# Squares of the gated tile: from GpSimd to the scalar engine in a state-space loop

## The reference, cut to what matters

```python
y = _ssd(x, Bm, Cm, D, dt, dt_bias)          # 128 heads of 64: 8192 channels
yg = y * jax.nn.silu(gate)
yg_g = yg.reshape(Bsz, S, NG, GROUP)         # 8 groups of 1024 channels
rstd = jax.lax.rsqrt(jnp.mean(jnp.square(yg_g), axis=-1, keepdims=True) + EPS)
out = (yg_g * rstd).reshape(Bsz, S, INTER) * norm_w
return out @ out_proj_w.T
```

## Time and profile before

| | |
|---|---|
| median of 3 runs | 2258.87 us (2258.38 to 2261.21) |
| the profiled execution | 2256.16 us, its span 2253.9 us |
| mean granted clock of PE | 0.987 of full speed |
| busy: PE, DVE, ACT, POOL | 2149.1, 1676.1, 1434.7, 1038.2 us |
| stages, us from the span's start | expert and attention blocks to about 550, first SwiGLU and the set-up of the loop to about 595, loop to about 2032, its end to about 2062, second SwiGLU to 2254 |

### The profile page before, as it was taken

One profiled execution on the slowest core, in us unless ns is written; L12 is line 12 of the kernel. 1 busy time (PEld: TensorE's weight loads), 2 busy tenths in 40 slices (PEclk: granted clock), 3 DMA queues, 4 the chain that ended last, 5 costly groups with the idle time before them and its releaser, 6 DMA issues. The chain is left out here.

```text
span 2253.9 us, 34737 instructions
## 1 busy us (share of the span) xinstructions
PE 2149.1 (95%) x12556; PEld 1748.4 (78%) x12556; DVE 1676.1 (74%) x2693; ACT 1434.7 (64%) x3086; POOL 1038.2 (46%) x759
## 2 busy tenths in 40 slices
PE   7889989999899999999999999999999999997999
PEld 7856677887688878878887887887887888785887
DVE  7667755133688898889889889889988988986221
ACT  4377734333877677677777767766877677673332
POOL 5466535443146344444435533634445443545442
PEclk9999999999999999999999999999999999998999
DMA  3000012331333233223322323223322322231332
GB/s 131 1 1 1 1 43 61 94 94 57 141 113 108 94 117 122 85 86 140 122 85 85 141 94 113 97 94 129 107 100 85 141 108 100 85 113 40 92 95 83
DMA packets 64151, 202.50 MB, mean 90 GB/s; under 512 B 7024, under 2 KB 8048, under 8 KB 55664
## 3 DMA queue, kind: packets, MB, share of 16 engines
q1 hardware_dynamic: 63984, 200.31, 25.9%
HBM read 197.39 MB, written 2.88 MB: 89 GB/s over the span
## 5 line engine op out<-in xcount | busy, mean ns | idle before, releaser
L529 POOL TENSOR_TENSOR wAl<-rawA,wAh 128x512 fp32r<-128x512 f32 x233 | 325.8, 1411 | 406.1 <-ACT wAh L670 405.4
L1599 PE MATMUL ps<-xTh,wAh 128*128 128x512 f32 x1512 | 427.3, 404 | 7.9 <-DVE oacc L1437 3.0
L1599 PE MATMUL ps<-xTl,wAh 128*128 128x512 f32 x1512 | 415.0, 396 | 0.0
L1599 PE MATMUL ps<-xTh,wAl 128*128 128x512 f32 x1512 | 413.9, 395 | 0.0
L1332 DVE SCALAR_TENSOR_TENSOR work<-ps,chp,work 128x510 f32<-128x510 f32 (+2 forms) x465 | 343.5, 744 | 51.6 <-ACT work L829 41.6
L1599 PEld LDWEIGHTS ps<-xTl,wAh 128*128 128x128 f32 x1512 | 284.9, 188 | 69.7
L1599 PEld LDWEIGHTS ps<-xTh,wAh 128*128 128x128 f32 x1512 | 276.6, 189 | 78.4 <-issue 17.5
L1599 PEld LDWEIGHTS ps<-xTh,wAl 128*128 128x128 f32 x1512 | 283.6, 188 | 69.3
L535 POOL TENSOR_TENSOR wBl<-rawB,wBh 128x512 fp32r<-128x512 f32 x108 | 142.2, 1330 | 386.1 <-ACT wBh L674 386.1
L866 ACT ACTIVATE eb<-eb,gc 128x128 f32<-128x128 f32 x1008 | 307.7, 391 | 18.0 <-DMA eb<-scr_decays 18.0
L579 POOL TENSOR_TENSOR sqt<-gt 128x512 f32<-128x512 f32 x112 | 154.4, 1379 | 120.6 <-DVE gt L1391 112.1
(11 more groups left out here) (202 smaller groups left out, 3958.5 us busy)
## 6 DMA issues: line engine op xcount, KB each, us to landing
eb<-scr_decays SPq DMA_DIRECT2D x63, 1536.0 KB, 6.4
rawA<-ma_in SPq DMA_DIRECT2D x144, 256.0 KB, 3.6
rawA<-fa_in SPq DMA_DIRECT2D x88, 256.0 KB, 2.6
rawB<-mb_in SPq DMA_DIRECT2D x64, 256.0 KB, 2.8
rawB<-fb_in SPq DMA_DIRECT2D x44, 256.0 KB, 2.6
x<-x_in SPq DMA_DIRECT2D x8, 256.0 KB, 6.2
x_out<-x SPq DMA_DIRECT2D x8, 256.0 KB, 2.7
wqraw<-wqkv_in SPq DMA_DIRECT2D x1, 1536.0 KB, 10.9
```

The source lines that it names most:

```text
L529: nc.gpsimd.tensor_tensor(wAl[:, slot, :], rawA[:, slot, :], wAh[:, slot, :].bitcast(F32), ALU.subtract).then_inc(A_lo, 1)
L1599: return nc.tensor.matmul(o, l, r, start=start, stop=end, **kw)
```

## The change

The squares leave POOL. A new function on ACT, `y_square`, writes them into `sqt` behind each `y_hi`, after a wait until POOL has added up the square before it. POOL's `square` only adds `sqt` to `sq` (or copies it, for v = 0). Two moves go with it: in odd steps POOL's `lo_B` pair goes from ahead of the two additions to behind them, and in `finish` the four `lo_A` and the `lo_B` for the second SwiGLU go from ahead of both squares to behind the second one. `y_lo`, `taps`, PE's order and all DMAs stay as they are.

```diff
--- before.py
+++ after.py
@@ -567,17 +567,13 @@
 
         def square(v, g, p):
 
-            pool.wait_ge(m_yg, 2 * (g * TPG + v) + p + 1 + FREE)
             half = slice(512 * p, 512 * p + 512)
-            y = gt[:, v % 2, half]
+            pool.wait_ge(m_sqt, 2 * (g * TPG + v) + p + 1)
             if v == 0:
                 pool.wait_ge(m_ss, g + FREE)
-                nc.gpsimd.tensor_tensor(sq[:, half], y, y, ALU.mult).then_inc(m_sq, 1)
+                nc.gpsimd.tensor_copy(sq[:, half], sqt[:, :]).then_inc(m_sq, 1)
             else:
-                k = g * 2 * (TPG - 1) + 2 * (v - 1) + p + 1
                 pool.wait_ge(m_sq, 2 * (g * TPG + v) + p + FREE)
-                nc.gpsimd.tensor_tensor(sqt[:, :], y, y, ALU.mult).then_inc(m_sqt, 1)
-                pool.wait_ge(m_sqt, k)
                 nc.gpsimd.tensor_tensor(sq[:, half], sq[:, half], sqt[:, :], ALU.add).then_inc(m_sq, 1)
 
         def rstd_of(g):
@@ -588,13 +584,13 @@
         def step(v, g, last=False, first=False):
             for i in step_tiles(v, last):
                 lo_A(A0G + i, g, NA_G)
-            if v % 2 == 1:
-                lo_B(B0G + v + 1, g, TPG)
-                lo_B(B0G + v + 2, g, TPG)
             if v == 0 and not first:
                 rstd_of(g - 1)
             square(v, g, 0)
             square(v, g, 1)
+            if v % 2 == 1:
+                lo_B(B0G + v + 1, g, TPG)
+                lo_B(B0G + v + 2, g, TPG)
 
         def last_rstd(p):
             pool.wait_ge(m_var, NG + p + FREE)
@@ -603,12 +599,12 @@
                                     ALU.pow).then_inc(m_rstd, 1)
 
         def finish():
+            square(TPG - 1, NG - 1, 0)
+            last_rstd(0)
+            square(TPG - 1, NG - 1, 1)
             for u in range(4):
                 lo_A(A0F + u)
             lo_B(B0F)
-            square(TPG - 1, NG - 1, 0)
-            last_rstd(0)
-            square(TPG - 1, NG - 1, 1)
             for t in range(AHEAD):
                 layer_rstd(5, t)
             last_rstd(1)
@@ -880,6 +876,12 @@
             nc.scalar.activation(yTh[:, v % 2, half], gt[:, v % 2, half], ACT.Copy,
                                  scale=param(0, 2 + 2 * v, 6)).then_inc(m_yhi, 1)
 
+        def y_square(g, v, p):
+            k = 2 * (g * TPG + v) + p
+            act.wait_ge(m_yg, k + 1 + FREE)
+            act.wait_ge(m_sq, k + FREE)
+            nc.scalar.activation(sqt[:, :], gt[:, v % 2, 512 * p:512 * p + 512], ACT.Square).then_inc(m_sqt, 1)
+
         def step(v, g, last=False, first=False):
 
             gn, todo = step_chunks(v, g, last)
@@ -912,7 +914,9 @@
                 conv_silu(gn, conv[1])
                 conv_start(gn, conv[3], slot)
                 y_hi(g, v, 0)
+                y_square(g, v, 0)
                 y_hi(g, v, 1)
+                y_square(g, v, 1)
                 conv_silu(gn, conv[2])
                 conv_start(gn, conv[4], slot)
                 conv_silu(gn, conv[3])
@@ -940,7 +946,9 @@
                 hi_A(A0F + u)
             hi_B(B0F)
             y_hi(NG - 1, TPG - 1, 0)
+            y_square(NG - 1, TPG - 1, 0)
             y_hi(NG - 1, TPG - 1, 1)
+            y_square(NG - 1, TPG - 1, 1)
             normalise(5, 0)
             for t in range(1, AHEAD):
                 normalise(5, t)
```

## The result

The changed kernel takes 2290.24 us (median of 4 runs, 2289.49 to 2290.47) against 2259.57 us (median of 4, 2258.38 to 2261.21): ratio 1.0135 (95% interval 1.0123 to 1.0148), 30.7 us slower. The profiled execution took 2290.11 us, its span is 2288.3 us, the mean granted clock 0.985.

A forecast was written before the change was run, and what follows sets the result against it. TensorE, busy 95% of the span, was taken as the bound. The terms 27 + 2 + 1.3 - 3 + 4 + 0 + 4 gave 35 us over 2258.87, so 2294 us, range 2265 to 2322.

The forecast's parts named there:

- odd steps v = 3 and 5: Steps v = 3 and v = 5 of eight groups: 1.7 us slower each, 27 us in all (bounds 6 and 42).
- step v = 1: First odd step: later in front, earlier at the decay pair; 2 us for groups 1 to 7, 1.3 for group 0.
- even steps: POOL's multiplications leave y_lo and decay_off, most of PE's waits for decay matrices go: -3 us.
- step v = 7: Squares between conv_start and conv_silu may make taps(3) and chunk 6 late: 0.6 us in 7 groups, 4 us.
- end of the loop: PE's sums start about 5 us sooner, but splits now stand ahead of layer_rstd: gain given back, 0 us.
- clock: New waits of PE bring part of the time at 1.2 GHz: 4 us added (bounds 0 and 15).
- The square between the two y_hi: ACT in odd steps: the square moves y_hi(1), and with it y_lo(1), by 0.6 us.
- The additions' new place: Odd steps, beside DVE: the first addition costs y_lo(1) 0.15 us, the second costs the decay_off pair 1.08 us.
- Only the order on ACT: Additions miss DVE's two-input instructions, only the square's 0.6 us counts in odd steps: 2271 us, chance 0.17.
- Faster: Additions fall into DVE's pauses, and DVE, freed from 112 multiplications beside it, shortens PE's waits: 2245 us, chance 0.11.
- No change: Small losses in odd steps made up by v = 1, even steps and the end: within 4.5 us of 2259, chance 0.09.
- ACT as the bound: 128 squares add 81 us to ACT, busy 1434.7 of 2254 us; counted inside the forecast, no chance of its own.

The follow-up runs named there:

- e1: Changed kernel with POOL's additions and copies into sq replaced by memsets that read nothing, the sums of squares left out: 2248.46 us, ratio 0.9955.
- e6: Kernel before with only the change's finish order (squares and last_rstd ahead of the four lo_A and the lo_B): 2257.22 us, ratio 0.9991.
- e7: Kernel before with finish reordered: squares and last_rstd first, each layer_rstd followed by one lo_A, lo_B last: 2254.46 us, ratio 0.9979.
- e4: Kernel before with only POOL's lo_B pair moved behind the squares in odd steps, all squares still on POOL: 2307.33 us, ratio 1.0220.
- e9: Changed kernel with both y_hi ahead of the first square on ACT in steps 1, 3 and 5: 2271.21 us, ratio 1.0050.
- e5: Changed kernel, odd steps: ACT's squares behind the exponentials and behind hi_B, POOL's lo_B pair between the additions: 2255.85 us, ratio 0.9986.
- e3: Changed kernel, steps 1, 3, 5: POOL's additions back behind the lo_B pair, ACT's second square behind hi_B, first square unmoved: 2277.56 us, ratio 1.0081.

## Why the prediction was right, step by step

The time, 2294 us, was 4 us above the measured one. The mechanism came out as written: the square ahead of y_hi(1), the addition beside decay_off, PE's new wait at t = 3 of steps 3 and 5, 16 times. The sum, 35 us, agrees with the 34.4 us between the two spans, but that is in part luck, since errors of both signs stand behind it:

| step of the prediction | priced | measured |
|---|---|---|
| odd steps v = 3 and 5 | 27 | 31.7: 1.63 a step in nine, 2.4 in seven |
| step v = 1, group 0 | 1.3 | 3.9 |
| step v = 1, groups 1 to 7 | 2 | -1.4 |
| even steps | -3 | -5.1 (-5.3 of it in v = 2) |
| step v = 7 | 4 | 4.4 |
| end of the loop | 0 | +0.1 |
| clock | 4 | about -3 in the loop, inside the rows above |

*The square between the two y_hi* was priced 0.6 and lasts 0.622 us. It moves y_hi(1) by only 0.51 (1.61 us behind y_hi(0), before 1.10) and the second y_lo by 0.52 against PE's first output product, where 0.6 or more had been written. PE's restart costs 0.10 (0.73 instead of 0.63), not 0.02. The two errors cancel: less the margin the square costs 0.47 us in e1, and the sum had 0.45.

*The additions' new place.* The second addition beside decay_off was priced 1.08: the pair went from 1.29 to 2.38 us, and stays at 1.29 in e1. The first was priced 0.15 and cost y_lo 0.08 us in v = 5. In seven of the eight steps v = 3 it cost 0.56 us (1.31 against 0.75), since DVE enters them late; these steps also had no margin left before the change, and the wait for the decay pair adds 0.31 us. Taking v = 5 as the pattern for v = 3 made this term too small by some 5.4 us; v = 5 itself was a little cheaper than priced (1.63 against 1.7), so in all it is 4.7 us short. The rows also show who waits for whom, which I had left open. In v = 5 the second addition starts at 1470.12, 0.33 us behind the decay_off pair, and ends at 1471.62; that it takes 1.50 us instead of 1.28 (the half of the B splits' 2.55) is its own wait for the first decay_off. The second decay_off ends at 1472.17, 0.55 us behind the addition. In v = 3 the first addition (1.81 us) ends at 1426.64 and the second y_lo at 1427.19, again 0.55 behind; in the earlier trace rows the addition ends at 1428.02 and y_lo at 1428.57, 0.55 too. It is so wherever a y_lo or decay_off is stretched and ends behind a 128x512 instruction of POOL (mostly an addition): 58 times in the kernel before and 93 times in the changed one, always 0.54 to 0.56 us. DVE's instruction thus gets on only when the addition is through. The Trainium skill has this as a rule (SBUF — State Buffer, the section SBUF: two separate sides: an exclusive lock on the shared pair of ports, held for the whole instruction, and for a VectorE instruction with two SBUF inputs only against a GpSimd instruction that reads SBUF). The rows above agree with it, and e1 with its last part: 0.75 and 1.29 us beside memsets. My estimate from it, 1.3 us for the pair, was too high by 0.2 all the same, since of the 0.75 us of a DVE instruction only 0.55 lie behind the addition's end.

*Step v = 1.* That DVE's sum decides was right. In group 4 of before PE waited 0.43 us at t = 3 and 1.92 at t = 7, together 2.35; the changed kernel's timeline has, in the same group, the two waits the other way round, 2.38 together:

```profile
1387.82 0.72 PE L1607 MATMUL ps<-wBh,yTh 128*128 128x512 f32 x2 [2.12 <-DVE oacc L1425]
1399.43 0.73 PE L1607 MATMUL ps<-wBh,yTh 128*128 128x512 f32 x2 [0.26 <-DVE oacc L1425]
```

The step is 28.95 us in both. Group 0 had no such wait and now has one of 2.02 us; its other 1.9 us are mostly clock, since the granted clock was 0.83 in the 10 us around it (second row below). The -1.4 us of the other groups are clock as well: before had four of them at a low clock, the changed kernel one.

*Even steps.* In v = 2 of group 4 a wait of 0.50 us for the decay matrices is gone, and so in two other groups; the wait list has 0.9 us in one place, against 2.5 in four. With PE's restarts these are 1.8 us of the 5.3, and the rest is clock. So what the change itself gave here is less than the 3 us priced.

*The clock* is the term with the wrong sign. I expected longer waits to bring more low clock. The windows of the changed kernel (us, busy us of PE, PEld, DVE, ACT, POOL, then PEclk; a value under 1.00 has a part at 1.2 GHz) show a stretch with a wait of 2.03 us at full clock, against 0.83 after the 1.97 us of the earlier trace rows:

```profile
1430.00:1440.00 10.00, 8.00 (x34) 6.47 (x35) 9.38 (x13) 6.24 (x15) 3.79 (x3) 1.00 0.00 1
...
632.00:642.00 10.00, 7.98 (x29) 6.00 (x27) 7.86 (x12) 4.66 (x8) 3.76 (x3) 0.83 0.00 0
```

Inside the loop, its last microseconds aside, before had four such stretches, each some 1.5 us of time (steps 1 and 2 of group 6 are 29.46 and 16.11 us, those of group 4 28.95 and 15.62, and 0.50 of the last is the decay wait, which group 6 lacks), the changed kernel two. Two other traces with the loop of before have four (e6) and five (e7), so one trace of each kernel says little about the size, and in e4 five of seven equal waits of 1.8 us in v = 3 were followed by the low clock and two were not. What decides whether a wait of 2 us brings the clock down no run here isolates; it stays open.

*Step v = 7* was priced as a mixture of two orders (y_lo first or addition first): 0.6 us in each of seven groups. It is a mixture: 0.9 us in five groups, where the addition catches y_lo, and nothing in the first two, where it does not (y_lo takes 0.74 us) and where PE waited at this place before the change already; together 4.4 us. The timeline of the changed kernel in step 7 of group 4 shows y_lo caught by the first addition, taps(3) behind it and chunk 6 late:

```profile
1513.03 1.29 POOL L577 TENSOR_TENSOR sq<-sq,sqt 128x512 f32<-128x512 f32 x1 [5.25 <-ACT sqt L883]
1513.13 1.74 DVE L1405 SCALAR_TENSOR_TENSOR yTl<-gt,chp,yTh 128x512 fp32r<-128x512 f32 x1
...
1514.79 2.30 DVE L1340 SCALAR_TENSOR_TENSOR work<-ps,chp,work 128x510 f32<-128x510 f32 x3
...
1517.24 1.17 PE L1607 MATMUL ps<-xTh,wAh 128*128 128x512 f32 x4 [0.64 <-DVE work L1340]
```

*The end of the loop* went as written, the gain given back in a second wait of PE; e6 shows it alone.

*The rivals.* "Only the order on ACT" is refuted by e9 and e4, which lose time in the odd steps without the square in front. "Faster" needed y_lo(1) less than 0.15 us late; it was 0.52 late. "No change" allowed 4.5 us, and it was 30.7. "ACT as the bound" is refuted by e5.

## What to carry to other kernels

Before work is moved between engines, look for the places where the bound engine nearly waits: in 16 steps it had 0.15 us of margin or none, that decided this change, and no total of busy time shows it. Look at each kind of step by itself: v = 3 and v = 5 run the same code, and the change cost 2.4 us in one and 1.6 in the other. Moving instructions past others on a half-idle engine can be dear (e4: 48.6 us for two instructions moved in each odd step), because it changes what they run beside. GpSimd's reads belong where VectorE works from PSUM or pauses (in e9 the second addition lies beside scale_x, which keeps its 0.68 and 0.41 us), and a producer with one buffer has to move together with its consumer (e3 against e5).

## What the runs showed that I had not expected

- The move of the B splits alone (e4, 48.6 us) is dearer than the whole change (30.7 us).
- Two waits of TensorE of the same 2 us, one with the granted clock at 1.00 around it and one at 0.83.
- That v = 3 and v = 5, the same code, differ: 26.19 against 26.00 us before, 28.59 against 27.63 after.
- That a y_lo or decay_off of VectorE that is caught by an instruction of GpSimd which reads SBUF ends 0.54 to 0.56 us behind it, in every one of the 151 cases of the two kernels; a GpSimd memset of 128x512 fp32 (0.53 us) at the same place delays nothing.
- The changed end of the loop saves 5 us of one wait and nothing of the time; the same splits placed between the row norms save 4 us (e7).
